# POOL drains behind each sixth indirect DMA instead of each sixteenth, and up to the last gather

## The reference

```python
h = (x_flat @ W_gat).reshape(M, HEADS, NUM_EXPERTS)
src = concatenate([edge_index[0], loops]); dst = concatenate([edge_index[1], loops])
e = leaky_relu(a_src[src] + a_dst[dst], 0.2)
ee = exp(e - segment_max(e, dst)[dst])
alpha = ee / (segment_sum(ee, dst)[dst] + 1e-16)
agg = segment_sum(h[src] * alpha[:, :, None], dst)
scores = layernorm(agg, ...).mean over heads        # top 2 of 4 experts, softmax
out = sum over experts of gate * (gelu(x @ W1 + b1) @ W2 + b2)
```

## Time and profile before

| what | value |
|---|---|
| median of the runs | 4237.11 us |
| span of the profiled execution | 5018.1 us |
| POOL busy in it | 2431.5 us, 48% |
| DVE busy | 2254.2 us, 45% |
| PE busy | 2170.6 us, 43% |
| POOL's edge gathers L790, busy | 2004.7 us in 2048 |

### The profile page before, as it was taken

The page is one execution under the profiler, slowest core; times in us unless marked ns, Lnnn a source line. Parts: engine busy times, 40 slices in busy tenths (PEclk is TensorE's granted clock), DMA queues, the critical chain, the costliest instruction groups (busy, mean ns, idle before and its releaser), DMA issues.

```text
span 5018.1 us, 28173 instructions
## 1 busy us (share of the span) xinstructions
PE 2170.6 (43%) x7631; PEld 912.4 (18%) x7631; DVE 2254.2 (45%) x3946; ACT 1178.5 (23%) x1734; POOL 2431.5 (48%) x2473
## 2 busy tenths in 40 slices
PE   0611278885456465556553143436564322000015
PEld 0211133332122121212111011112222111000014
DVE  8899867763336263635346531315140102101235
ACT  0300145552223232323222121224243312000001
POOL 0000162656653626161636666662636554777562
PEclk9955589987677676777766576678686656555557
DMA  3200044432223222322313221212122212011124
GB/s 87 39 1 0 21 73 76 74 71 46 37 52 65 37 61 46 64 41 46 61 19 68 35 49 28 56 34 63 41 68 55 64 34 87 10 24 22 31 47 145
DMA packets 652065, 247.84 MB, mean 49 GB/s; under 512 B 552276, under 2 KB 632708, under 8 KB 649476
## 3 DMA queue, kind: packets, MB, share of 16 engines
q1 hardware_dynamic: 573988, 216.76, 18.3%
q0 software_dynamic: 77920, 29.29, 5.8%
HBM read 152.68 MB, written 91.71 MB: 49 GB/s over the span
## 4 chain that ended last, share of the span: by engine, by line
PE 23%; another core or an unknown queue 20%; DVE 19%; issue 16%; POOL 8%; DVEq 7%; ACT 5%; DMA 2%; SPq 1%; ACTq 0%; POOLq 0%
POOL ring L790 8%; DVE res L1298 4%; PE ps L887 4%; DVEq L1300 4%; PE ps L877 2%; PE ps L991 2%; PE ps L902 2%; PE ps L1002 2%; PE ps L1013 1%; DVE res L1633 1%; DMA arena<-xnT 1%; PE ps L1052 1%; DVE arena L1659 1%; PE ps L950 1%
## 5 line engine op out<-in xcount | busy, mean ns | idle before, releaser
L790 POOL DMA_INDIRECT ring<-table,src_i x2048 | 2004.7, 979 | 1587.0 <-issue 883.0
L887 PE MATMUL ps<-arena,w 64*128 64x448 f32 x896 | 293.8, 740 | 441.5 <-issue 197.9
L754 POOL DMA_INDIRECT ring<-keys_d,place x128 | 138.8, 1084 | 653.8 <-DVEq L1255 589.5
L991 PE MATMUL ps<-arena 64*128 64x512 f32 x800 | 238.5, 710 | 360.2 <-DMA arena<-xnT 221.6
L1013 PE MATMUL ps<-ident,arena 128*128 128x128 f32 x800 | 156.1, 354 | 466.4 <-issue 272.7
L1805 DVE TENSOR_TENSOR arena<-ps,arena 128x1024 f32<-128x1024 f32 x68 | 83.3, 1225 | 594.9 <-remote 410.8
L902 PE MATMUL ps<-arena,w 128*64 128x448 f32 x896 | 247.7, 683 | 237.3 <-issue 237.3
L1645 DVE TENSOR_TENSOR arena<-arena,ps 128x448 f32<-128x448 f32 x297 | 174.8, 618 | 364.9 <-issue 195.7
L1186 ACT ACTIVATE arena<-ps,arena 128x1024 f32<-128x1024 f32 x200 | 217.0, 1115 | 256.6 <-remote 120.3
L1659 DVE TENSOR_TENSOR_SCAN arena<-ps,carry,arena 128x448 f32<-128x448 f32 x122 | 130.8, 1131 | 320.6 <-issue 178.0
L1105 ACT ACTIVATE ps<-ps,tb 128x448 f32<-128x448 f32 x297 | 171.9, 605 | 359.7 <-PE ps L887 154.9
(11 more groups left out here) (338 smaller groups left out, 3968.8 us busy)
## 6 DMA issues: line engine op xcount, KB each, us to landing
arena<-in_x SPq DMA_DIRECT2D x304, 110.0 KB
ring<-table,src_i POOLq DMA_INDIRECT x2048
partial<-res SPq DMA_DIRECT2D x15, 1536.0 KB
arena<-in_x SPq DMA_DIRECT2D x160, 140.0 KB
outputs_d<-arena SPq DMA_DIRECT2D x32, 512.0 KB
arena<-outputs_d SPq DMA_DIRECT2D x32, 512.0 KB
arena<-xnT SPq DMA_DIRECT2D x100, 128.0 KB
arena<-h_tok SPq DMA_DIRECT2D x50, 256.0 KB
```

The source lines that it names most:

```text
L790: g.indirect_dma_start(out=ring[k % 2][:, j - FROM[k], :], out_offset=None, in_=table[0:GRAPH_NODES, :], in_offset=off(ap=src_i[:, j:j + 1 ...
L887: mm(bank(1 + (2 * i + z) % 3)[:, 0:CHUNK], w2[lower_upper(z), i * P:(i + 1) * P], h1[lower_upper(z), :], start=True, stop=True).then_inc( ...
L991: m = mm(hid[ee % 2][:, z * NT:(z + 1) * NT], fw1[lower_upper(z), ee, :], xf[q][lower_upper(z), :], start=True, stop=True)
```

## The change

Two numbers that `rest` uses are changed. The drain stands ahead of every gather or scatter whose number leaves 5 when divided by 6, and the limit is the number of columns, so it never ends. The edge gathers then have 341 drains (21 or 22 in each chunk of 128, 16 in the chunk of 96, 5 in the last), the block gathers 21, the early scatters 19. No other instruction is added, removed or moved, and no engine but POOL has a changed queue.

```diff
 GROUP = 4
-BURST = 16
-BURSTS_UNTIL = 1536
+BURST = 6
+BURSTS_UNTIL = COLS
```

## The result

The changed kernel takes 4791.76 us (four runs, 4787.59 to 4799.27) beside 4238.16 us of the kernel before (four runs, 4235.48 to 4243.43): a ratio of 1.1302, with a 95% interval of 1.1286 to 1.1318. The prediction was 4770 us.

What follows compares the result with a forecast made beforehand. POOL was taken to bound the timed runs from about the first edge gather on: 4237.1 + 622 (245 added drains at 2.54 us) - 89 (a wait filled) = 4770 us, 12.6% slower, range 4150 to 4880 us.

Steps and rivals of the forecast that it cites:

- POOL bounds the timed runs: From about the first edge gather on, POOL's queue sets the time of the timed runs; chance 0.58, 4770 us.
- The price of a drain: POOL's edge gathers: 2.54 us for each of 245 added drains, 622 us in all.
- The bare stretch: Chunks 13 to 16, only gathers left: 64 added drains without cover lengthen the kernel by 163 us.
- The slack of 89 us: POOL's wait of 89.0 us before chunk 13's first gather, filled by a later POOL and so subtracted.
- Search and scatters at nothing: Block gathers (13 more drains, 33 us) and early scatters (12, 30 us): nothing in the sum, 32 us in the upper end.
- The 11.43 us of cover at L776: Before the first edge gather: 11.4 us of slack behind the block gathers and early scatters.
- What a drain gives: Pauses on POOL every 10.0 instead of 22.5 us let PE's results through sooner; worth nothing while POOL bounds.
- Rival A: Faster: POOL's instructions shorter in timed runs, PE's late results real; 4173 us, 1.5% faster; chance 0.21.
- Rival B: Slower by less: POOL's ring waits at L1637 cover all but chunks 13 to 16; 4400 us; chance 0.14.
- Rival C: No difference: relief of PE takes off as much as chunks 13 to 16 add; chance 0.07.
- The signs in the profile after: What the changed kernel's profile would show: gaps, chunk times, waits, matmul rate, and a span of 4850 to 5000 us.

Runs made afterwards that it cites:

- the second profile of the kernel before: The kernel before, unchanged, run and profiled again: 4234.52 us measured, profiled span 4232.6 us.

## Why the prediction was right, point by point

**POOL bounds the timed runs: right**, and the forecast hung on it. It was inferred from the median, which left no room for the ring waits of the earlier trace rows; the second profile of the kernel before shows that there are none.

**The price of a drain: too high.** The term was 245 x 2.54 = 622 us. From the second profile of before to the profile after, the stretch from first to last edge gather grew from 2932 us (1049.5 to 3981.6) to 3459 us (1083.4 to 4542.5), by 527 us: 2.15 us for each drain added. The step that failed took the gap of a burst of 16 for that of a burst of 6. The price falls with the burst, so 341 cheaper drains replace 96 dearer ones. The bare stretch alone shows it: predicted 163 us more, measured 628.9 - 496.0 = 133 us for 64 drains, 2.08 us each. Ten gathers fewer in a burst, at the 0.041 us each measured above, make 0.41 us of the price.

**The slack of 89 us: not there.** In the second profile chunk 13's first gather follows chunk 12's last without a ring wait, because the pairs had ended long before (PE is idle in all of chunk 12). The 89.0 us in the earlier trace rows belong to the longer execution.

**Search and scatters at nothing: wrong.** The first edge gather moved from 1049.5 to 1083.4 us, 34 us, just above the 32 us that the range kept for it; done alone, 26 us of time. Some 5 of the 34 us are not the drains': the wait for DVE ahead of the first block gather was 595.1 us after and 589.8 in the second profile of before, and it lies at either value in the other profiles. The 11.43 us of cover at L776 in the earlier trace rows belong to the longer execution; in the second profile that wait is 0.30 us.

The sum by measured terms: 527 + 34 - 2 (the end, 248.6 after and 250.6 to 251 before) = 559 us, the distance of the two spans (4791.1 and 4232.6). The prediction's 533 came close by luck: a drain priced too high (95 us too much) and a slack that did not exist (89 us) nearly cancelled. That POOL bounds, and that each added drain is paid in full, was not luck.

**What a drain gives: wrong.** "A drain costs POOL time and gives PE time" rested on the earlier trace rows; without drains the pairs end earlier, not later (3026.7 and 3240.3 us). Rival A had this as its ground, and fell with it. Rival B's cover, the ring waits, was that of the one execution. Rival C needed either.

**The signs in the profile after.** Idle time near 2.84 us ahead of every sixth gather: 2.43 at the median. Chunks of 210 to 220 us: 206 to 225, and 232 for the first, which has the ten scatters behind it. "Issue" idle near 1480 us: 1436.9. DVE's waits far above 374.5: 1469.7. The last four chunks near 675 us: 628.9. No ring waits, no waits at "remote". More matmuls per us beside a gathering chunk: wrong against the second profile of before, chunk 2 has the same 492 in 222.4 us in place of 190.1. A profiled span of 4850 to 5000 us: wrong, 4791.1, in step with its runs, since this execution has nothing of what lengthened the first.

By the Trainium skill, DMA: Bandwidth & Descriptors, section "Anatomy of one DMA — SWDGE (gpsimd) path", the fixed cost of such a DMA is about 2.0 us, and by that the sum had been 4638 us as an estimate. The traces agree in that a gather lands 2.3 us after its start and the drain waits for that landing. The price comes near the 2.0 us for the shortest burst (2.07 us) and leaves it with longer ones (3.11 us at 32), by the part that follows the landing.

## What to carry to other kernels

Compare the span of a profile with the median of the runs before trusting a wait in it: where the span is much longer, take the waits out and see whether what remains of the busiest queue still fits in the median. A pause on an engine is paid in full where that engine's queue runs through (here POOL's, until all drains were gone), however many others seem to gain by it; measure the kernel without the pause before tuning how often it comes. And the price of a drain at one spacing is not its price at another: here one part is the wait for the last transfer, and another grows with the transfers since the drain before.

## What the runs showed of the hardware

A drain on POOL behind indirect DMAs costs 2.07 us in bursts of 2 and 3.11 us in bursts of 32, and a second one right behind it some 0.15 us. It holds POOL until the last DMA before it has landed (2.3 to 2.5 us after that DMA's start at the median); POOL's next DMA follows 0.83 us after that landing in bursts of 2 and 2.05 us after it in bursts of 32. Without drains, indirect DMAs of 128 rows follow each other on POOL in 1.25 us, and a chunk of 128 takes 165 us in the bare stretch and 165 to 175 us beside the work of PE, ACT and DVE (the first, with ten scatters behind it, 181).

One profiled execution of the kernel before was 781 us longer than its runs, with PE's results late by 13 us and more while POOL was gathering; none of the other profiles has a wait at "remote", with bursts of 2, 6, 16 or 32 or without a drain. What set that execution apart stays open: it was not tried to bring it back. Its trace also holds only 23202 semaphore updates, where the others hold 64976 to 65408, so many of its waits at "remote" may be waits whose end was not recorded; that alone does not explain the longer span.
